# One product for both inner products with v3 and its broadcast row, in the Householder steps of a four-mixer kernel

## What is computed

```python
def _L3_gnn_ref(features, A, W1, b1, W2, b2):
    deg = jnp.sum(A, axis=0) + jnp.sum(A, axis=1) - jnp.diagonal(A)
    d_inv_sqrt = jnp.where(deg > 0, jax.lax.rsqrt(deg), 0.0)
    L_norm = d_inv_sqrt[:, None] * (jnp.diag(deg) - A) * d_inv_sqrt[None, :]
    _, U = jnp.linalg.eigh(L_norm)
    agg = jnp.einsum('mn,bnd->bmd', U.T, features)
    out = jax.nn.relu(agg @ W1 + b1) @ W2 + b2
    return jnp.einsum('nm,bmd->bnd', U, out)
```

## Time and profile before

| | |
|---|---|
| median of 3 runs | 1161.13 us |
| lowest to highest | 1157.04 to 1161.92 us |
| the profiled execution | 1159.08 us |
| its span | 1157.4 us |
| instructions | 14411 |
| busy: TensorE, VectorE, ScalarE, POOL | 878.6, 832.3, 476.3, 224.8 us |

### The profile page before, as it was taken

The page is one execution under the profiler, slowest core; times in us unless marked ns, Lnnn a source line. Parts: engine busy times, 40 slices in busy tenths (PEclk is TensorE's granted clock), DMA queues, the critical chain, the costliest instruction groups (busy, mean ns, idle before and its releaser), DMA issues.

```text
span 1157.4 us, 14411 instructions
## 1 busy us (share of the span) xinstructions
PE 878.6 (76%) x4032; PEld 613.0 (53%) x4038; DVE 832.3 (72%) x3265; ACT 476.3 (41%) x1047; POOL 224.8 (19%) x716
## 2 busy tenths in 40 slices
PE   4699989999999999999996457665275165665398
PEld 3588854555557666655556345444253044454265
DVE  6867778877777888777769766764867887556633
ACT  0058755544333444434340133342134155565275
POOL 2111111111111111111110110100211211888000
PEclk9999999999999999999996555555555588999599
DMA  7000000000000000000000000000000000000022
GB/s 246 1 1 1 1 1 1 1 1 1 0 1 1 1 1 1 2 0 1 1 1 1 0 1 1 1 0 1 0 0 1 0 1 1 1 1 1 0 73 73
DMA packets 13974, 12.21 MB, mean 11 GB/s; under 512 B 1091, under 2 KB 10822, under 8 KB 13894
## 3 DMA queue, kind: packets, MB, share of 16 engines
q1 hardware_dynamic: 10704, 8.46, 2.2%
q10 hardware_dynamic: 3190, 2.84, 0.7%
HBM read 7.10 MB, written 4.19 MB: 10 GB/s over the span
## 4 chain that ended last, share of the span: by engine, by line
issue 44%; PE 18%; DVE 16%; POOL 15%; ACT 6%; POOLq 0%; DVEq 0%; ACTq 0%
PE bank L495 16%; POOL col_root L322 7%; POOL t L354 2%; ACT T L398 2%; DVE X L711 2%; POOL PP L354 2%; DVE HT L710 2%; ACT T L459 2%; POOL u L354 2%; PE bank L505 2%; DVE stat L718 1%; POOL XI L326 1%; DVE tt L710 1%; DVE m L1039 1%; ACT sg L478 1%
## 5 line engine op out<-in xcount | busy, mean ns | idle before, releaser
L442 ACT ACTIVATE G<-bank,bias 128x512 f32<-128x512 f32 (+1 forms) x252 | 159.8, 635 | 248.7 <-PE bank L495 247.8
L495 PE MATMUL bank<-HT,wih 128*128 128x512 f32 (+1 forms) x504 | 248.3, 579 | 0.5 <-ACT HT L428 0.5
L402 ACT COPY T<-bank 128x512 f32<-128x512 f32 x144 | 83.6, 581 | 259.5 <-PE bank L495 226.3
L322 POOL TENSOR_TENSOR col_root<-sa,neg_half 128x1 f32<-128x1 f32 x126 | 79.3, 629 | 491.4 <-DVE sa L712 491.4
L495 PE MATMUL bank<-H,whh 128*128 128x512 f32 (+1 forms) x288 | 135.7, 553 | 0.0
L398 ACT ACTIVATE T<-X,nbias,rstd 128x128 f32<-128x128 f32 x256 | 104.3, 485 | 18.6 <-DVE nbias L711 18.6
L505 PE MATMUL bank<-ident,T 128*128 128x128 f32 x256 | 57.0, 363 | 54.3 <-ACT T L459 30.2
L495 PEld LDWEIGHTS bank<-HT,wih 128*128 128x128 f32 x504 | 80.1, 193 | 10.1 <-issue 3.8
L495 PEld LDWEIGHTS bank<-ST 128*128 128x128 f32 x254 | 47.8, 203 | 71.2 <-DVE ST L710 43.4
L505 PEld LDWEIGHTS bank<-ident,T 128*128 128x128 f32 x256 | 37.7, 182 | 86.2 <-ACT T L459 50.8
L711 DVE SCALAR_TENSOR_TENSOR X<-bank,sm,X 128x128 f32<-128x128 f32 x128 | 36.0, 344 | 54.7 <-PE bank L495 54.3
(11 more groups left out here) (324 smaller groups left out, 1895.1 us busy)
## 6 DMA issues: line engine op xcount, KB each, us to landing
out_x<-T SPq DMA_DIRECT2D x16, 256.0 KB, 2.3
wih<-in_WihT ACTq DMA_DIRECT2D x1, 1024.0 KB
whh<-in_WhhT ACTq DMA_DIRECT2D x1, 1024.0 KB
qkvT<-in_WqkvT ACTq DMA_DIRECT2D x1, 192.0 KB
wg<-in_Wg ACTq DMA_DIRECT2D x2, 64.0 KB
l3w<-in_L3W ACTq DMA_DIRECT2D x2, 64.0 KB
adjT<-in_adjT ACTq DMA_DIRECT2D x1, 64.0 KB
adj<-in_adj SPq DMA_DIRECT2D x1, 64.0 KB, 1.9
```

Of the source, the lines that this page charges most:

```text
L322: e.tensor_tensor(out=col["root"][:, :], in0=sa[:, 0:1], in1=neg_half[:, :], op=ALU.pow).then_inc(root_ready, 1)
L402: e.copy(out=dst[:, :], in_=src[:, :]).then_inc(done, 1)
L442: e.activation(G[x.h][:, gate, 0:n], gate_bank(k)[:, 0:n], ACT.Tanh if gate == 2 else ACT.Sigmoid, bias=bias[:, 4 * (x.p - 1) + gate:4 * ( ...
L495: mm = lambda out, l, r, start=True, stop=True: e.matmul(out, l, r, start=start, stop=stop)
```

## The change

The products with p and with v3 become one. Its left side is v3 (now a tile of its own), its right side the columns y, p and the rest of twice the identity, which stand side by side in a new tile `VI` of 130 columns: step i writes u, y into columns i, i+1, then v, p into i, i+2, so that column i keeps v, and columns from i+3 on are still twice the identity. The product gives v3.y, v3.p and the row of 2 v3 in `bank1[4:]`, P+1-i columns in place of 2 and P-i-1. q is formed as v (v3.p) - p, the next `XI` as 2 v (v3.y) - y (so `xy` needs v and y, not v3; `low12` has its halves exchanged). The wait for v3 ahead of `xy`, the wait for `vr_ready` ahead of A1 and the wait of TensorE for `p_ready` go. V is `VI[:, 0:P]`, its last two columns are cleared after the steps by a memset on VectorE, where a memset on POOL cleared `ST` at the start. POOL fills `VI` with one more add ahead of `low12`; TensorE and VectorE wait for 8 constants in place of 7 at the start.

```diff
--- before.py
+++ after.py
@@ -194,15 +194,16 @@
         bank = [ctx.enter_context(nc.psum_tensor(f"bank{i}", [P, 512], F32)) for i in range(8)]
 
 
-        ident, ident2, low, upper, sup, ones, iota_f, limit_row = [sb(n, [P, P]) for n in "ident ident2 low upper sup ones iota_f limit_row".split()]
+        ident, low, upper, sup, ones, iota_f, limit_row = [sb(n, [P, P]) for n in "ident low upper sup ones iota_f limit_row".split()]
+        VI, ident2 = sb("VI", [P, P + 2]), sb("ident2", [P, P])
         low12 = sb("low12", [P, P, 2])
         identb = sb("identb", [P, P], BF16)
         half, neg_half, grid, limit = sb("half", [P, 1]), sb("neg_half", [P, 1]), sb("grid", [P, POINTS[0]]), sb("limit", [P, 1])
 
         adj, A, A1, Ln = [sb(n, [P, P]) for n in "adj A A1 Ln".split()]
         XI = [sb(f"XI{i}", [P, 5]) for i in range(2)]
-        ST, GAM = sb("ST", [P, P, 5]), sb("GAM", [P, P])
-        V = ST[:, :, 2]
+        GAM, v3 = sb("GAM", [P, P]), sb("v3", [P, 1])
+        V = VI[:, 0:P]
         sa, xy = sb("sa", [P, 3]), sb("xy", [P, 2, 2])
         col = {n: sb("col_" + n, [P, 1]) for n in (
             "deg rowsum diag pos inv dinv root c a1 rec q sgm mxe mxd mnd lo w cnt1 frac d_at d_up lam mn idx ss inr lmax sign gcol").split()}
@@ -249,8 +250,8 @@
         out_done = [sem("out_done0"), sem("out_done1")]
         s_pool, s_const, identb_ready = sems("s_pool s_const identb_ready")
         deg_ps, dinv_in, dinv_rt, dinv_rep, ln_r, ln_t = sems("deg_ps dinv_in dinv_rt dinv_rep ln_r ln_t")
-        x_ready, a_ready, oh_ready, s_ready, gx_ready, sa_ready, root_ready, p_ready, k_ready, v3_ready, vr_ready, q_ready, wr_ready = sems(
-            "x_ready a_ready oh_ready s_ready gx_ready sa_ready root_ready p_ready k_ready v3_ready vr_ready q_ready wr_ready")
+        x_ready, a_ready, oh_ready, s_ready, gx_ready, sa_ready, root_ready, p_ready, k_ready, v3_ready, q_ready, wr_ready = sems(
+            "x_ready a_ready oh_ready s_ready gx_ready sa_ready root_ready p_ready k_ready v3_ready q_ready wr_ready")
         td_in, td_rep, wy_ps, wy_sb, wy_v = sems("td_in td_rep wy_ps wy_sb wy_v")
         m_ready, dl_ready, p_done, pr_ready, sgn_ready, sum_ps, hist_in, hist_ps = sems(
             "m_ready dl_ready p_done pr_ready sgn_ready sum_ps hist_in hist_ps")
@@ -297,21 +298,21 @@
             e.memset(minus[:, :], -0.5).then_inc(s_pool, 1)
             e.memset(tiny[:, :], 1e-30).then_inc(s_pool, 1)
             e.memset(neg_half[:, :], -0.5).then_inc(s_pool, 1)
-            e.memset(ST[:, STEPS:P, :], 0.0).then_inc(s_pool, 1)
             e.memset(GAM[:, STEPS:P], 0.0).then_inc(s_pool, 1)
             e.iota(iota_f[:, :], pattern=[[1, P]], base=0, channel_multiplier=0, allow_small_or_imprecise_dtypes=True).then_inc(s_pool, 1)
             e.iota(limit[:, :], pattern=[[0, 1]], base=-P, channel_multiplier=2, allow_small_or_imprecise_dtypes=True).then_inc(s_pool, 1)
             e.iota(limit_row[:, :], pattern=[[2, P]], base=-P, channel_multiplier=0, allow_small_or_imprecise_dtypes=True).then_inc(s_pool, 1)
             e.iota(grid[:, :], pattern=[[1, POINTS[0]]], base=0, channel_multiplier=POINTS[0], allow_small_or_imprecise_dtypes=True).then_inc(s_pool, 1)
-            e.wait_ge(s_pool, 11)
+            e.wait_ge(s_pool, 10)
             for t, op, base, cm, st in ((ident, ALU.is_equal, 0, 1, -1), (low, ALU.is_gt, 0, 1, -1), (upper, ALU.is_gt, 0, -1, 1), (sup, ALU.is_equal, -1, -1, 1)):
                 e.affine_select(out=t[:, :], in_=ones[:, :], compare_op=op, fill=0.0, base=base, pattern=[[st, P]], channel_multiplier=cm).then_inc(s_const, 1)
             e.wait_ge(s_const, 4)
             e.tensor_copy(out=identb[:, :], in_=ident[:, :]).then_inc(identb_ready, 1)
             e.tensor_copy(out=XI[0][:, 2:3], in_=ident[:, 1:2]).then_inc(oh_ready, 1)
             e.tensor_tensor(out=ident2[:, :], in0=ident[:, :], in1=ident[:, :], op=ALU.add).then_inc(s_const, 1)
-            e.tensor_copy(out=low12[:, :, 0], in_=low[:, :]).then_inc(s_const, 1)
-            e.tensor_tensor(out=low12[:, :, 1], in0=low[:, :], in1=low[:, :], op=ALU.add).then_inc(s_const, 1)
+            e.tensor_tensor(out=VI[:, 2:P + 2], in0=ident[:, :], in1=ident[:, :], op=ALU.add).then_inc(s_const, 1)
+            e.tensor_tensor(out=low12[:, :, 0], in0=low[:, :], in1=low[:, :], op=ALU.add).then_inc(s_const, 1)
+            e.tensor_copy(out=low12[:, :, 1], in_=low[:, :]).then_inc(s_const, 1)
             e.wait_ge(dinv_in, 1)
             e.tensor_tensor(out=col["root"][:, :], in0=col["inv"][:, :], in1=half[:, :], op=ALU.pow).then_inc(dinv_rt, 1)
             e.wait_ge(dinv_rep, 1)
@@ -510,7 +511,7 @@
 
 
             e.wait_ge(c_adj, 16)
-            e.wait_ge(s_const, 7)
+            e.wait_ge(s_const, 8)
             mm(bank[0][:, 0:1], adj[:, :], ones[:, 0:1]).then_inc(deg_ps, 1)
             e.wait_ge(dinv_rep, 1)
             mm(bank[1][:, 0:P], bc(col["dinv"][:, 0:1]), ident[:, :]).then_inc(dinv_rep, 1)
@@ -589,10 +590,8 @@
                     mm(bank[1][:, 0:2], A[:, :], xi[:, 0:3:2]).then_inc(gx_ready, 1)
                 window(3 * i)
                 if i < STEPS:
-                    e.wait_ge(p_ready, i + 1)
-                    mm(bank[0][:, 4:6], bc(ST[:, i, 3:4]), ST[:, i, 0:3:2]).then_inc(k_ready, 1)
                     e.wait_ge(v3_ready, i + 1)
-                    mm(bank[1][:, P + i + 1:2 * P], bc(ST[:, i, 4:5]), ident2[:, i + 1:P]).then_inc(vr_ready, 1)
+                    mm(bank[1][:, 4:P + 5 - i], bc(v3[:, 0:1]), VI[:, i + 1:P + 2]).then_inc(k_ready, 1)
                 window(3 * i + 1)
                 if i < STEPS:
                     e.wait_ge(q_ready, i + 1)
@@ -601,7 +600,7 @@
 
 
             e.wait_ge(l_h, len(UNITS))
-            e.wait_ge(td_in, 2)
+            e.wait_ge(td_in, 3)
             mm(bank[3][:, 0:2 * P], ones[:, :], W01[:, :]).then_inc(td_rep, 1)
             mm(bank[0][:, 0:P], V, V).then_inc(wy_ps, 1)
             e.transpose(bank[1][:, 0:P], V, ident[:, :]).then_inc(wy_ps, 1)
@@ -894,8 +893,8 @@
             for i in range(FIRST_MIXER_STEPS):
                 hh = i < STEPS
                 if hh:
-                    xi, st, gam, rest = XI[i % 2], ST[:, i, :], GAM[:, i:i + 1], slice(i + 1, P)
-                    u_y, v_p, v, p, v3 = st[:, 0:2], st[:, 2:4], st[:, 2:3], st[:, 3:4], st[:, 4:5]
+                    xi, gam, rest = XI[i % 2], GAM[:, i:i + 1], slice(i + 1, P)
+                    u_y, v_p, v, p = VI[:, i:i + 2], VI[:, i:i + 3:2], VI[:, i:i + 1], VI[:, i + 2:i + 3]
 
                     e.wait_ge(s_ready, i + 1)
                     TS(sa[:, :], bank[0][:, 0:3], 1e-30, None, ALU.add).then_inc(sa_ready, 1)
@@ -913,29 +912,28 @@
                     k = link.note(STT(gam, sa[:, 1:2], 1e-30, c("rec"), ALU.is_gt, ALU.mult))
                     e.wait_ge(ch_e, k)
                     e.wait_ge(p_ready, i + 1)
-                    TS(v3, v, gam, 0.5, ALU.mult, ALU.mult).then_inc(v3_ready, 1)
-                    e.wait_ge(v3_ready, i + 1)
+                    TS(v3[:, :], v, gam, 0.5, ALU.mult, ALU.mult).then_inc(v3_ready, 1)
                     if i < STEPS - 1:
-                        m = link.note(TT(xy[:, :, :], st[:, 1:5:3].unsqueeze(1).to_broadcast([P, 2, 2]), low12[:, i + 1:i + 3, :], ALU.mult))
+                        m = link.note(TT(xy[:, :, :], u_y.unsqueeze(1).to_broadcast([P, 2, 2]), low12[:, i + 1:i + 3, :], ALU.mult))
                 first_mixer(i, 1)
                 if hh:
                     e.wait_ge(k_ready, i + 1)
-                    STT(c("q"), v3, bank[0][:, 5:6], p, ALU.mult, ALU.subtract).then_inc(q_ready, 1)
+                    STT(c("q"), v, bank[1][:, 5:6], p, ALU.mult, ALU.subtract).then_inc(q_ready, 1)
                     if i < STEPS - 1:
                         e.wait_ge(ch_e, m)
-                        STT(XI[(i + 1) % 2][:, 0:2], xy[:, :, 1], bank[0][:, 4:5], xy[:, :, 0], ALU.mult, ALU.subtract).then_inc(x_ready, 1)
+                        STT(XI[(i + 1) % 2][:, 0:2], xy[:, :, 0], bank[1][:, 4:5], xy[:, :, 1], ALU.mult, ALU.subtract).then_inc(x_ready, 1)
                     e.wait_ge(q_ready, i + 1)
-                    e.wait_ge(vr_ready, i + 1)
-                    link.note(STT(A1[:, rest], bank[1][:, P + i + 1:2 * P], c("q"), A[:, rest], ALU.mult, ALU.add))
+                    link.note(STT(A1[:, rest], bank[1][:, 6:P + 5 - i], c("q"), A[:, rest], ALU.mult, ALU.add))
                     a = link.n
                 first_mixer(i, 2)
                 if hh:
                     e.wait_ge(ch_e, a)
                     e.wait_ge(wr_ready, i + 1)
-                    STT(A[:, rest], bank[7][:, rest], v3, A1[:, rest], ALU.mult, ALU.add).then_inc(a_ready, 1)
+                    STT(A[:, rest], bank[7][:, rest], v3[:, 0:1], A1[:, rest], ALU.mult, ALU.add).then_inc(a_ready, 1)
                     e.wait_ge(a_ready, i + 2)
 
 
+            e.memset(VI[:, STEPS:P], 0.0).then_inc(td_in, 1)
```

## The result

The changed kernel's median is **1165.91 us** (20 runs, 1158.47 to 1170.61), the kernel before beside it 1159.63 (20 runs, 1154.08 to 1163.05): a ratio of 1.0049, interval 1.0034 to 1.0063, so +5.7 us (the medians themselves are 6.3 apart).

The account below looks back on a forecast made before the run. It took two side-by-side loops, TensorE's and VectorE's, to bound the Householder steps, whichever is late in a stage. Terms 0.3 + 2.5 + 0 - 0.5 + 0 + 1.4 + 0.8 + 0.05 = +4.6 us gave 1165.7 us, range 1158 to 1171.5.

Parts of the forecast that it names:

- constants: Program start: one more POOL add, which VectorE's first instruction waits for, delays everything by +0.3 us (bounds 0 to +0.40).
- steps 0 to 9: First ten Householder steps: q waits for the wide product and starts later, +2.5 us in sum.
- steps 10 to 29: Graph-layer steps: ScalarE's copy ends last and q has over a microsecond of slack; small costs and gains cancel, 0.
- wide product's end + 0.05: Every step: q's new start, 0.04 us behind the wide product's end plus two more columns.
- First part: First LSTM part, steps 30 to 45: `xy` moves up without its wait, gaining 0.03 us a step, -0.5 us.
- Second part: Steps 46 to 67: pairs losing 0.07 and steps waiting on TensorE gaining 0.14 cancel, 0 (between -1.5 and +1.5 us).
- Third part: Steps 68 to 100: eight steps without an LSTM product ahead of q lose 0.2 us each; sum +1.4 us.
- Fourth part: Steps 101 to 125, in pairs: twelve pairs lose by q's later start, +0.8 us.
- the pair loses +0.07: Steps 101 to 125: TensorE wins 0.14 us, but later q and A1 make each pair 0.07 us longer.
- TensorE rival: TensorE's queue bounds all over, so about 85 steps gain 0.14 us each: sum -9, 1152 us; chance 0.07.
- clock rival: TensorE's clock falls again in steps 68 to 100: 1168.7 us for one fall, 1171.7 for two; chance 0.19.
- Every later stage just shifts: Everything behind the Householder steps only moves in time, adding nothing to the +4.6 us.

Follow-up runs that it names:

- mixed form: Changed kernel with separate early and late products restored in the 40 steps without an LSTM product ahead of q: 1159.76 us, ratio 1.0004 to the kernel before.
- second: Changed kernel, nothing edited, run and profiled once more: 1163.18 us, ratio 1.005 to the kernel before.
- late constant: Changed kernel with the add that fills `VI` moved behind `low12`, VectorE waiting for it only ahead of the first `XI`: 1164.61 us, one profiled execution.
- cut: Changed kernel ended behind the Householder steps, x written out there, all later stages left out: 627.90 us.
- long execution: Changed kernel, nothing edited, one more profiled execution: 1169.64 us.
- dummy product: Changed kernel with an unread two-column product in place of the removed product with p: 1174.18 us, ratio 1.011 to the kernel before.
- fillers: Unread 128-column products ahead of the first step and in steps 0-9, 26-28, 68: mixed form with `VI` filled late 1151.43 us; kernel before 1158.02 us.
- cut kernel before: Kernel before the change, ended behind the Householder steps, x written out there, all later stages left out: 621.73 us.

## Why the prediction was right or wrong

The time (1165.91 for 1165.7) and the sign (+0.49%, just inside the half per cent) came out, and the mechanism, q's wait for the wide product, is shown by the mixed form. That the time came out to 0.2 us is luck. The base was 1.5 too high (1161.13, the median of three runs, for 1159.63), and the change 1.7 larger than forecast (6.3 between the medians for 4.6); the steps of the profiles explain about half of it, the rest lies behind the steps, where nothing was forecast; and the median stands at the edge of the gap between two groups of times. The table has the first profile's steps less those of before, and the lowest and highest over four further profiles of the changed form (second, late constant, cut, long execution; the late constant's first row left out).

| term | predicted | first profile | the others |
|---|---|---|---|
| constants | +0.3 | +0.32 | +0.27 to +0.34 |
| steps 0 to 9 | +2.5 | +3.11 | +3.11 to +3.13 |
| steps 10 to 29 | 0 | +0.31 | -1.60 to 0.00 |
| steps 30 to 45 | -0.5 | -0.49 | -0.63 to -0.49 |
| steps 46 to 67 | 0 | -0.79 | -0.81 to -0.68 |
| steps 68 to 70 | in the next | +1.10 | +0.79 to +0.95 |
| steps 71 to 100 | +1.4 | +0.72 | +0.71 to +1.14 |
| steps 101 to 124 | +0.8 | -0.35 | -0.87 to -0.25 |
| all steps | +4.6 | +3.93 | +1.6 to +3.6 |

Pauses of VectorE are in these rows. Without them the first profile has -0.73 in steps 30 to 45, -0.55 in 46 to 67, +1.23 in 71 to 100 and -0.39 in 101 to 124.

- **Constants: right**, and tested alone.
- **Steps 0 to 9: mechanism right, size short.** Steps 0 to 5 and 7 lose 0.26 to 0.35 each, most 0.33, where I had 0.2 to 0.25. The term "wide product's end + 0.05" was mis-sized: q starts 0.11 behind the end in steps 1 to 5. And step 1 was no good example: q stood 0.91 behind v3 there before, but 0.84 in steps 2 to 5. Step 9 lost 0.67 for 0.7, step 8 0.21 for 0.3.
- **Steps 10 to 29: right** but for the clock: in the first profile steps 11 and 12 won 1.3, as the clock rose 10.6 us behind the `sa` of step 10 and not 12.8 as before, and step 28, where the clock fell, lost 1.5. The prediction's "granted clock is 1.00 from start to 600 us" read the 9s ahead of 75 us as a clock; the trace has no record there, and the weight loads (0.55 for two, as in the fall at 342.8) show the lower level. "Its passes are slow" was right, and this is why.
- **First part: mechanism right, size short**: 0.05 a step where I had 0.03, through the wait ahead of `xy`. The sum of -0.49 for -0.5 came out because a pause in step 44 took 0.25 back. Here the Trainium skill ("VectorE: DVE Perf Modes", "The DRAIN you can't avoid") was weighed, which measured a chain of copies in which the semaphores cost nothing extra. The trace does not agree for these small instructions: 0.13 without the wait, 0.24 with it, and the steps follow.
- **Second part: the term was too small.** Steps 46, 52, 58 and 64 gave back 0.07 to 0.09 at TensorE's queue (with the dummy product they take 4.55, changed 4.36 to 4.37). Steps 50, 56 and 62 gave back 0.10 each through the wait ahead of `xy` (with it put back they are at 4.74 to 4.77 again, as before), which the prediction had left out here. Step 48 lost its pause, 0.24, and the pairs lost 0.02, not 0.07.
- **Third part: right**, +1.23 for +1.4 without the pauses: the eight steps lose 0.15 to 0.21 each (82: 4.16 to 4.35), +1.4 together. The row shows +0.72 because steps 72 and 84 gave back 0.25 each. TensorE was not the bound there: with the dummy product they stay at 4.60 and 4.14. They had a pause of VectorE before and have none now.
- **Fourth part: the failed step**, "the pair loses +0.07". The wide product took 0.33, not 0.37, so q is 0.05 to 0.06 late, not 0.11; and A1, which had followed q by 0.30 with two waits, follows by 0.28 with one. What is left is 0.02 a pair, and there are ten such pairs, not twelve. Steps 101, 102 and 116 gave back 0.18, 0.19 and 0.10 at TensorE's queue (with the dummy product they take 4.55 again), which the prediction counted at nothing, and step 114 0.08 through the wait ahead of `xy`. So the part won 0.39 (without the pauses) where +0.8 was forecast.
- **The TensorE rival** (-9) was wrong as a whole, but its 0.14 is real where TensorE comes late: the dummy product costs 0.2 there. The change takes it away with q's wait. The 0.16 a step estimated from the Trainium skill ("TensorE: Matmul & The Clock Gate", "Back-to-back issue gap") is near what the dummy costs in bound steps (0.17 to 0.20) and near what steps 101 and 102 gave back, and far from the 0.02 that the pairs lost.
- **The clock rival** came true in part. No further fall appeared in the third part, but the one that is there lasts 13.7 us in all seven profiles of the changed form, and 10.2 in both of the old one without fillers: +0.8 to +1.1. With the dummy product, so with as many products as before, it lasts 13.7 too, so the count of products alone does not explain it; with five products more in step 68 it is gone in the mixed form. The fall at step 28 is no mark of the change: three of the seven have it, and the cut kernel before too (6.55 us for the step).
- **Missing from the forecast** was that the tail can move the median. "Every later stage just shifts" failed: same code, 547.9 to 557.3 us. The steps of the five changed profiles end 2.8 us later on average (3.93, 3.61, 2.04, 1.58 and 2.90), so about half of the +5.7 is of the steps. The rest is of the tail, and no run shows whether the change has a part in it.

## What to carry to other kernels

Merging two small products saves one only if its reader doesn't need the part that could be had early: before merging, write down for each reader what is late next, stage by stage, and keep both forms where the stages differ. Where a program runs partly at a lower granted clock, compare the time up to the last changed instruction as well as the whole, and profile several executions before a difference under 1% is put down to an edit. A few dummy products in the one place where the clock falls can be worth more than the edit itself, but each place has to be tried, also in both forms of the kernel.

## What the runs showed of the hardware

- TensorE runs at its lower level, 1.2 GHz, until 69 to 80 us in the kernels without fillers: most weight loads take 333 ns, as in the stretches granted 0.50, and 190 behind that point. The trace has no clock record ahead of it, and the profile prints 1.00. With fillers at the start (mixed form) loads take 333 ns until 5.1 us and 190 from the first record on, which is 1.00 at 5.4 us; from 12.2 to 73.6 us the records have 0.50, and loads take 333 again. So a printed 1.00 at the start of a kernel has to be checked against the loads and passes themselves.
- VectorE pauses for 0.24 to 0.37 us at a few places, the same ones in every profiled execution of one kernel, others in some changed programs (step 84 above). A difference of 0.25 in a single step can be this and nothing else.
- A reader of a product on VectorE starts 0.04 us behind its modelled end in steps 9, 82 and 113, but 0.11 in steps 1 to 5.
- Two small products in TensorE's stream are 0.14 us apart, and one more costs 0.17 to 0.20 a step where TensorE is the bound.
- The tail of one and the same program takes 547.9 or 557.3 us, with 314 or 361 us of it at the lower level.
